# Attention in a new order: the products of x and of the output in one bank, queries ahead of the shifts, inputs transposed ahead of the probabilities

## The reference

```python
x = x + tanh(g_xattn) * xattn(layernorm(x), ctx)     # 16 heads of 8; rope on k and v; softmax; Wp, bp
x = x + tanh(g_ffn) * moe(layernorm(x))              # 8 experts, top 2 of a gate, hidden 256
# xattn: q = x Wq', k = rope(c Wk'), v = rope(c Wv'); softmax(q k' / sqrt(8)) v, then Wp' and + bp
# moe:   top 2 of x @ gate; softmax of the two; sum of weight * (silu(x w0) * (x w1)) @ wo
```

## Time and profile before

| | us |
|---|---|
| median of 3 executions | 569.37 (568.95 to 570.17) |
| profiled execution | 569.16 |
| its span | 567.4 |

### The profile page before, as it was taken

The page is one execution under the profiler, slowest core; times in us unless marked ns, Lnnn a source line. Parts: engine busy times, 40 slices in busy tenths (PEclk is TensorE's granted clock), DMA queues, the critical chain, the costliest instruction groups (busy, mean ns, idle before and its releaser), DMA issues.

```text
span 567.4 us, 20235 instructions
## 1 busy us (share of the span) xinstructions
PE 538.1 (95%) x5964; PEld 457.0 (81%) x5965; DVE 401.5 (71%) x1356; ACT 411.9 (73%) x1083; POOL 378.5 (67%) x520
## 2 busy tenths in 40 slices
PE   8999999999999999999999998799999999999960
PEld 6888887788887887887887878699999999999950
DVE  5888988898998899899899865433333333335763
ACT  4788888888888888889998885356666666666630
POOL 3236777767767677776776767777766666666770
PEclk9999999999999999999999999899999999999995
DMA  3832121121212212122221124333333333337997
GB/s 88 239 121 75 55 81 58 56 74 61 79 56 71 68 51 79 56 61 72 68 76 56 52 69 143 104 100 109 98 93 93 93 93 94 94 90 208 314 317 222
DMA packets 70246, 57.96 MB, mean 102 GB/s; under 512 B 8966, under 2 KB 66062, under 8 KB 70192
## 3 DMA queue, kind: packets, MB, share of 16 engines
q1 hardware_dynamic: 52672, 35.98, 22.3%
q0 software_dynamic: 8640, 16.93, 9.0%
q10 hardware_dynamic: 8880, 4.39, 2.6%
HBM read 29.84 MB, written 24.15 MB: 95 GB/s over the span
## 4 chain that ended last, share of the span: by engine, by line
PE 86%; issue 4%; POOL 3%; DMA 2%; DVE 2%; ACT 1%; POOLq 0%; SPq 0%; ACTq 0%; DVEq 0%
PE psH L548 18%; PE psO L520 12%; PE psH L460 11%; PE psH L446 7%; PE psH L452 7%; PE psK L498 5%; PE psO L562 5%; PE psG L562 4%; PE psO L478 3%; PE psX L465 3%; PE psO L492 3%; POOL results L1134 2%; PE psX L502 1%; PE psK L473 1%; PE psX L503 1%
## 5 line engine op out<-in xcount | busy, mean ns | idle before, releaser
L1134 POOL DMA_INDIRECT results<-ys,zin x142 | 141.9, 999 | 55.1 <-issue 51.0
L1085 POOL DMA_INDIRECT lists<-zp,dest x128 | 128.5, 1004 | 62.5 <-DVE dest L889 32.6
L548 PE MATMUL psH<-zT,wcur 128*128 128x256 f32 x568 | 136.0, 383 | 0.0
L548 PEld LDWEIGHTS psH<-zT,wcur 128*128 128x128 f32 x568 | 103.3, 192 | 11.4
L994 DVE TENSOR_TENSOR hm<-psH,hs 128x512 f32<-128x512 f32 x71 | 49.1, 692 | 85.9 <-PE psH L548 51.4
L627 ACT ACTIVATE ex<-psH,rs 128x512 f32<-128x512 f32 x128 | 81.2, 684 | 39.0 <-PE psH L452 39.0
L874 DVE TENSOR_REDUCE mx<-psH 128x8 fp32r<-128x512 f32 x128 | 82.4, 686 | 4.5 <-PE psH L446 0.3
L520 PEld LDWEIGHTS psO<-v,pT 128*64 128x64 f32 x2048 | 64.9, 138 | 25.1 <-issue 23.1
L460 PE MATMUL psH<-ident,ex 128*128 128x128 f32 x512 | 76.5, 282 | 0.1
L520 PE MATMUL psO<-v,pT 128*64 128x64 f32 x2048 | 73.7, 225 | 0.6 <-ACT pT L631 0.6
L1116 POOL TENSOR_TENSOR kvr<-ropA,ropB 128x256 f32<-128x256 f32 x64 | 46.5, 726 | 40.3 <-DVE ropB L951 24.0
(11 more groups left out here) (157 smaller groups left out, 991.6 us busy)
## 6 DMA issues: line engine op xcount, KB each, us to landing
zin<-lists SPq DMA_DIRECT2D x71, 130.0 KB, 2.1
yy<-results SPq DMA_DIRECT2D x16, 512.0 KB, 5.5
xres<-x1r SPq DMA_DIRECT2D x32, 128.0 KB, 2.2
out_dram<-xres ACTq DMA_DIRECT2D x16, 256.0 KB, 3.6
xring<-in_x_dram SPq DMA_DIRECT2D x31, 128.0 KB, 2.2
cring<-in_ctx_dram SPq DMA_DIRECT2D x31, 128.0 KB, 2.4
results<-ys,zin POOLq DMA_INDIRECT x142, 2.3
lists<-pad SPq DMA_DIRECT2D x16, 130.0 KB, 2.5
```

The costliest lines, as they stand in the source:

```text
L548: last = pe.matmul(bank[t.buf(2)][:, k * ET:(k + 1) * ET], wcur[:, t.buf(2), a, k * P:(k + 1) * P], zT[:, t.buf(2), :], start=True, stop=True)
L1085: nc.gpsimd.indirect_dma_start(lists, bass.IndirectOffsetOnAxis(ap=dest[:, t.buf(4), j:j + 1], axis=0), zp[:, t.buf(4), j, :], None).then_ ...
L1134: nc.gpsimd.indirect_dma_start(results, bass.IndirectOffsetOnAxis(ap=zin[:, t.buf(8), h, D:D + 1].bitcast(U32), axis=0), ys[:, t.buf(8), h ...
```

## The change

Nothing that is computed changes. Moved, on TensorE: the shift of half 1 goes from the end of a step to the next step, between the query product and the shift of half 0, so the query product now comes ahead of both shifts; the transposes of the inputs go from behind k and v to ahead of the probabilities' transposes; x·idg goes behind them; the output product goes behind k and v; the counting matmuls go ahead of P·V. Exchanged banks: x·idg and the output product write psG instead of psO; the transpose of `on` and the counting matmuls write psO instead of psG, beside P·V. So x·idg waits for x1_done of the tile before and no more for `on`, and P·V waits for the copy oT of the tile before in place of x1_done. On ACT the copy qT goes ahead of the exponentials, xcT from the end of the step to between oT and pT. On DVE the sum x1r goes from ahead of the rope products to between the reciprocal and `on`; each fourth step `place` stands there and the sum behind `on`. In the experts psY is exchanged so that the first tile uses psG.

```diff
-        psZ, psY = [psX, psK], [psO, psG]
+        psZ, psY = [psX, psK], [psG, psO]
@@ TensorE
-                    pe.matmul(psG[:, 384:384 + 4 * E], lower[:, :], chosen[:, :, :], start=True, stop=False)
-                    pe.matmul(psG[:, 384:384 + 4 * E], allone[:, :], before[:, :, :], start=False, stop=True).then_inc(place_ps, 4)
+                    pe.matmul(psO[:, 384:384 + 4 * E], lower[:, :], chosen[:, :, :], start=True, stop=False)
+                    pe.matmul(psO[:, 384:384 + 4 * E], allone[:, :], before[:, :, :], start=False, stop=True).then_inc(place_ps, 4)
...
+                    if t := ATT_PE.at(s, 2):
+                        if static(s, -2):
+                            busy(6)
+                        wait_for(pe, mx_done[1], t)
+                        shift(1)
                     if t := ATT_PE.at(s, 2):
                         wait_for(pe, mx_done[0], t)
                         shift(0)
...
                     if t := ATT_PE.at(s, 1):
                         wait_for(pe, on_done, t)
-                        if static(s, -1):
-                            pe.wait_ge(logit_ready, 4)
-                        pe.matmul(psO[:, 368:368 + XW], xcT[:, t.buf(8), 0:P], idg[:, :], start=True, stop=False, skip_group_check=True)
...
-                        pe.transpose(psG[:, 0:P], on[:, t.buf(2), :], ident[:, :]).then_inc(oT_ps, 1)
+                        pe.transpose(psO[:, 256:384], on[:, t.buf(2), :], ident[:, :]).then_inc(oT_ps, 1)
+                    if t := ATT_PE.at(s, 5):
+                        rows_in(pe, t)
+                        wait_for(pe, q_sb, t, back=1)
+                        pe.transpose(psX[:, 0:P], xring[:, t.buf(4), :], ident[:, :])
+                        pe.transpose(psX[:, P:2 * P], cring[:, t.buf(4), :], ident[:, :]).then_inc(xc_ps, 1)
+                    if t := ATT_PE.at(s, 1):
+                        if static(s, -1):
+                            pe.wait_ge(logit_ready, 4)
+                        wait_for(pe, x1_done, t, back=1)
+                        pe.matmul(psG[:, P:P + XW], xcT[:, t.buf(8), 0:P], idg[:, :], start=True, stop=False, skip_group_check=True)
                     if t := ATT_PE.at(s, 2):
                         wait_for(pe, exp_done[1], t)
                         turn(t, 1)
                     if t := ATT_PE.at(s, 2):
                         wait_for(pe, exp_done[0], t)
                         turn(t, 0)
-                    if t := ATT_PE.at(s, 1):
-                        wait_for(pe, oT_sb, t)
-                        pe.matmul(psO[:, 368:368 + XW], oT[:, t.buf(2), :], wTg[:, :], start=False, stop=True, skip_group_check=True).then_inc(attn_ps, 1)
                     if t := ATT_PE.at(s, 4):
...
                         pe.matmul(psK[:, 0:2 * D], xcT[:, t.buf(8), P:2 * P], wT[:, 1:3, :], start=True, stop=True).then_inc(kv_ps, 1)
-                    if t := ATT_PE.at(s, 5):
-                        rows_in(pe, t)
-                        wait_for(pe, q_sb, t, back=1)
-                        pe.transpose(psX[:, 0:P], xring[:, t.buf(4), :], ident[:, :])
-                        pe.transpose(psX[:, P:2 * P], cring[:, t.buf(4), :], ident[:, :]).then_inc(xc_ps, 1)
+                    if t := ATT_PE.at(s, 1):
+                        wait_for(pe, oT_sb, t)
+                        pe.matmul(psG[:, P:P + XW], oT[:, t.buf(2), :], wTg[:, :], start=False, stop=True, skip_group_check=True).then_inc(attn_ps, 1)
...
                         scores(t, 0)
+                    if (t := ATT_PE.at(s, 0)) and t.buf(4) == 3 and not static(s, NT - 1):
+                        places(t)
...
                     if t := ATT_PE.at(s, 2):
                         wait_for(pe, v9_done, t)
-                        wait_for(pe, x1_done, t, back=1)
+                        wait_for(pe, oT_sb, t, back=1)
...
                         last.then_inc(pv_ps, 1)
-                    if (t := ATT_PE.at(s, 0)) and t.buf(4) == 3 and not static(s, NT - 1):
-                        places(t)
...
-                    if t := ATT_PE.at(s, 3):
-                        if static(s, -3):
-                            busy(6)
-                        wait_for(pe, mx_done[1], t)
-                        shift(1)
@@ ScalarE
+                    if t := ATT_ACT.at(s, 0):
+                        wait_for(act, q_ps, t)
+                        wait_for(act, s_ps[0], t, back=2)
+                        nc.scalar.copy(qT[:, t.buf(2), :], psX[:, 2 * P:3 * P]).then_inc(q_sb, 1)
                     if t := ATT_ACT.at(s, -2):
                         wait_for(act, shift_ps[1], t)
...
-                    if t := ATT_ACT.at(s, 0):
-                        wait_for(act, q_ps, t)
-                        wait_for(act, s_ps[0], t, back=2)
-                        nc.scalar.copy(qT[:, t.buf(2), :], psX[:, 2 * P:3 * P]).then_inc(q_sb, 1)
                     if t := ATT_ACT.at(s, -3):
                         wait_for(act, oT_ps, t)
                         wait_for(act, attn_ps, t, back=2)
-                        nc.scalar.copy(oT[:, t.buf(2), :], psG[:, 0:P]).then_inc(oT_sb, 1)
+                        nc.scalar.copy(oT[:, t.buf(2), :], psO[:, 256:384]).then_inc(oT_sb, 1)
+                    if t := ATT_ACT.at(s, 1):
+                        wait_for(act, xc_ps, t)
+                        wait_for(act, attn_ps, t, back=8)
+                        nc.scalar.copy(xcT[:, t.buf(8), :], psX[:, 0:2 * P]).then_inc(xc_sb, 1)
                     if t := ATT_ACT.at(s, -2):
                         wait_for(act, p_ps[1], t)
...
-                    if t := ATT_ACT.at(s, 1):
-                        wait_for(act, xc_ps, t)
-                        wait_for(act, attn_ps, t, back=8)
-                        nc.scalar.copy(xcT[:, t.buf(8), :], psX[:, 0:2 * P]).then_inc(xc_sb, 1)
@@ VectorE
+                def first_sum(t):
+                    wait_for(dve, attn_ps, t)
+                    wait_for(dve, zn_done, t, back=4)
+                    wait_slot(dve, [x1_out[i // 2] for i in range(4)], t, 16, back=4)
+                    nc.vector.tensor_tensor(x1r[:, t.buf(4), :], psG[:, P:P + XW], bpg[:, :], ALU.add).then_inc(x1_done, 1)
...
                         nc.vector.reciprocal(rden[:, :], o[:, :, DH]).then_inc(rden_done, 1)
+                    r = (r if (r := ATT_DVE.at(s, -1)) and r.buf(4) == 3 else None)
+                    if r:
+                        rows(r)
+                    elif t := ATT_DVE.at(s, 0):
+                        first_sum(t)
+                    if t := ATT_DVE.at(s, 1):
+                        o = psO[:, 0:PAIRS * VW].rearrange("p (h w) -> p h w", w=DH + 1)
                         wait_for(dve, rden_done, t)
...
+                    if r and (t := ATT_DVE.at(s, 0)):
+                        first_sum(t)
```

More of the change, by code:

```diff
@@ L429, in places @@
                     wait_for(pe, place_done, t, back=4)
-                    pe.matmul(psG[:, 384:384 + 4 * E], lower[:, :], chosen[:, :, :], start=True, stop=False)
-                    pe.matmul(psG[:, 384:384 + 4 * E], allone[:, :], before[:, :, :], start=False, stop=True).then_inc(place_ps, 4)
+                    pe.matmul(psO[:, 384:384 + 4 * E], lower[:, :], chosen[:, :, :], start=True, stop=False)
+                    pe.matmul(psO[:, 384:384 + 4 * E], allone[:, :], before[:, :, :], start=False, stop=True).then_inc(place_ps, 4)
                 def count():
-                    pe.matmul(psG[:, 0:E], allone[:, :], before[:, 0, :], start=True, stop=True).then_inc(count_ps, 1)
+                    pe.matmul(psO[:, 416:416 + E], allone[:, :], before[:, 0, :], start=True, stop=True).then_inc(count_ps, 1)
                 def busy(n):
@@ L795, in first_table @@
                         dve.wait_ge(count_ps, 1)
-                        nc.vector.tensor_scalar(early[:, 0, :], psG[:, 0:E], 0.0, None, ALU.add).then_inc(early_table, 1)
+                        nc.vector.tensor_scalar(early[:, 0, :], psO[:, 416:416 + E], 0.0, None, ALU.add).then_inc(early_table, 1)
                         dve.wait_ge(early_table, 1)
@@ L824, in second_table @@
                         dve.wait_ge(count_ps, 2)
-                        nc.vector.tensor_copy(cnt[:, :], psG[:, 0:E]).then_inc(late_table, 1)
+                        nc.vector.tensor_copy(cnt[:, :], psO[:, 416:416 + E]).then_inc(late_table, 1)
                         dve.wait_ge(late_table, 1)
@@ L937, in attention_step @@
                         nc.vector.tensor_tensor(chosen[:, :, :], oh[:, :, 0, :], oh[:, :, 1, :], ALU.add).then_inc(chosen_done, 4)
-                    if t := ATT_DVE.at(s, 0):
-                        wait_for(dve, attn_ps, t)
-                        wait_for(dve, zn_done, t, back=4)
-                        wait_slot(dve, [x1_out[i // 2] for i in range(4)], t, 16, back=4)
-                        nc.vector.tensor_tensor(x1r[:, t.buf(4), :], psO[:, 368:368 + XW], bpg[:, :], ALU.add).then_inc(x1_done, 1)
                     if t := ATT_DVE.at(s, 3):
```

16 lines of the change are left out of this document (8 added, 8 removed).

## The result

| us | before | after |
|---|---|---|
| median | 569.47 (568.95 to 570.17, 4 executions) | 589.16 (588.97 to 590.97, 4 executions) |
| ratio | 1 | 1.0352, interval 1.0329 to 1.0375 |
| span of the profiled execution | 567.4 | 587.4 |

The change costs 19.7 us. Forecast were 11.6 us, 580.8, with a range up to 589.0. So the direction came as forecast, and the size did not: the time lies just beyond the upper end. Three later sets of runs took about 93 us longer (663 us) with every kernel, the one before too, so their numbers stand apart, under 8 of the experiments.

A forecast was written before the change was run, and what follows sets the result against it. The prediction took ACT's exponentials, then TensorE's own queue, to bound the attention step. It summed 569.2 + 3.6 (ordinary steps) + 8.0 (counting matmuls) = 580.8 us, range 571 to 589.

The forecast's parts named there:

- The bound: Attention step of 5.01 us: ACT's exponentials set it up to the second transposes, TensorE's queue behind; their 0.16 stall stays.
- Queries ahead of the shifts: TensorE, attention: the query product now delays the shift of half 1, +0.22 us a step.
- Inputs ahead of the probabilities: TensorE, attention: 0.22 leaves the paid stretch, only 0.16 got back; period 5.07, +0.06 a step, +3.6 to 3.8 us.
- xcT ahead of pT: ACT, attention: the second copy pT starts 0.00 to 0.03 us later; upper end 0.25 a step without overlap.
- Counts ahead of P·V: TensorE, every fourth step: counting matmuls wait for GpSimd's `before`, 0.61 or 0.45 us a group, 8.0 in all.
- my split into eight and seven: Counting groups in attention: eight cost 0.61 us each and seven 0.45, from earlier slack of 0.51 or 0.67.
- The start: No term of its own; remaining terms of either sign, under 1.5 us, were set to zero.
- Banks, `on`: TensorE, attention: x·idg stops waiting for `on`, whose transpose waits about 0.1 us instead, under the exponentials; gain nothing.
- The sum x1r: DVE, attention: moved behind the reciprocal, it makes `on` up to 0.04 us later, under the exponentials; costed at nothing.
- Experts: Experts' phase: order kept, psO and psG exchanged, cost 0.
- rival 3: ACT, attention: no overlap, pT 0.25 us later each step; 592 us, half of it 586; larger loss, chance 0.13.
- the count's own upper end: Counting groups in attention: GpSimd's chain not earlier, 0.23 us more each, 11.5 in all instead of 8.0.

The follow-up runs named there:

- 8 of the experiments: Eight timings of kernels with parts of the change or related edits, beside a kernel before of 662 to 663 us; all slower than it by 1 to 4%.
- experiment 1: The kernel after, with the counting matmuls back behind P·V and writing psK: 577.82 us, ratio 1.0152.
- experiment 2: The kernel after, with ACT's copy xcT back behind the two copies pT: 587.05 us, ratio 1.0313.
- experiment 3: The kernel after, with both the counting matmuls back behind P·V (into psK) and xcT behind pT: 575.14 us, ratio 1.0118.
- experiment 4: The kernel before, with only the query product ahead of both shifts and its copy qT ahead of the exponentials: 585.22 us, ratio 1.0282.
- experiment 5: The kernel before, with only the exchanged banks, x·idg behind the transpose of `on` and the moved sum x1r; counts behind P·V in psK: 571.8 us, ratio 1.0039.
- experiment 6: The kernel before, with only the counting matmuls moved ahead of P·V: 582.77 us, ratio 1.025.

## Why the prediction was right or wrong

- *The bound.* Right. The stall of 0.16 ahead of the second transposes is there in the ordinary steps of the kernel after as in those of the one before, and in experiments 1 to 6.
- *Queries ahead of the shifts, +0.22.* Right: 0.23 alone (experiment 4).
- *Inputs ahead of the probabilities, 0.16 of 0.22 got back, period 5.07.* Right: 5.07 stands in experiments 2 and 3, where xcT is out of the way.
- *xcT ahead of pT, 0.00 to 0.03, taken at nothing in the sum.* Mis-sized: this is the first step that failed. It costs 0.07 in each ordinary step (5.14 with it, 5.07 without, experiment 2). pT starts at +2.09 (reckoned +2.07); the second copy starts 0.04 later than before, near what I reckoned, but also takes 0.63 instead of 0.59, and ends at +3.19 to +3.20 instead of +3.13. Behind the exponential of half 0 ACT had no slack, and TensorE waits for ACT's last copy in each ordinary step, so every hundredth there is paid; the steps with a count are as long without it (experiment 2). Over the 44 steps: 5.61 measured, 2.6 forecast (44 × 0.06), 3.0 too little. Experiment 2 gives 2.25 of the 3.0 back; most of the rest lies in the steps behind a count, as in experiment 3.
- *Counts ahead of P·V, 0.61 and 0.45 a group.* The mechanism is right, place and releaser too; the sizes are short, and this is the second step that failed. Against the kernel before I forecast 0.67 and 0.51 more per counting step and measured 0.80 in both kinds, up to 1.1 in the last groups (6.54 instead of 5.40). Of what is missing (0.13 and 0.29), 0.09 to 0.12 are that P·V comes 0.21 to 0.24 behind the count, not 0.15, and q 0.03 later. In five of the 15 groups the count's load comes 0.23 behind the end of `before` and not 0.07, 0.16 more (in one other, 0.12). The timelines call that "issue"; the records of TensorE's own queue (line 104, `wait_for`), which they leave out, show why the two kinds differ. In the five groups a register operation (ALU_OP, at 194.40 in one) stands between the end of the wait for `before` (194.34) and the load (194.49); in the others none does, and the load follows the end of the wait by 0.025. The cheaper kind of my split into eight and seven has only these five groups. Sum: 12.40 measured, 8.9 forecast (15 × 0.59), 3.5 too little.
- *The start.* Not forecast: a term that I put at nothing. At the fifth tile the kernel after is 2.05 late, of which four steps of the forecast 0.06 explain 0.24. 0.93 lie in these four steps, most of it in the first, 5.54 instead of 4.87; experiment 4 has 5.52 there, so that goes with the queries ahead of the shifts. The other 1.12 lie before the first shift, and can be chance: kernels that start like the one before have it anywhere from 12.34 to 13.90, and one and the same kernel (the counts alone) at 12.34, 13.09 and 13.68.
- *Banks, `on`, 0.* Right: the ordinary step is 5.01 in experiment 5. *The sum x1r, 0.* Wrong in part: moved ahead of `kmask`, it costs 2.0 us alone and about 0.7 in experiment 3, in the steps behind a count. In the change the wait for pT hides most of it.
- *Experts, 0.* Right: the last shift is 20.07 later, the span 20.0.

The forecast by parts was 2.6 + 8.9 + 0.24 = 11.7. Measured were 5.6 + 12.4 + 2.05 = 20.1. The three misses (3.0, 3.5, 1.8) all have the same sign, which my range hadn't allowed for: its upper end came from rival 3 at half its price, and from the count's own upper end. Rival 3 (pT 0.25 later) holds in kind and falls in size: 0.07 to 0.10.

The Trainium skill, TensorEngine Tiling (Array Packing), Key Properties, has TensorE drain when the tiling mode changes. No run here can show a price for that. The load of the other shape comes 0.21 to 0.24 behind the count and the load of the same shape 0.04, but between the count and P·V the queue also passes two waits of P·V's own, which elsewhere pass while the scores run, and in every group P·V loads 0.025 behind the end of the second. So what I had too small there may well be the queue's time for two waits, and that the rows agree with the rule, as the prediction says, isn't shown.

## What to carry to other kernels

Ask of each move not only what it costs, but in which stretch of the step the instruction stands: the same 0.22 of TensorE is free under the exponentials, as long as there is slack, and paid in full behind them. A small instruction that waits for a slow engine belongs behind everything that others wait for; two counting matmuls ahead of P·V cost 11 to 13 us of 569. And where a copy on the path has no slack, give its neighbours their full price: errors of some hundredths in a loop of 60 add up, and here they all lay on one side.

## What the runs showed of the hardware that I had not expected

- Two semaphore waits that stand between two matmuls in TensorE's queue go with a gap even when little or nothing has to be waited for: P·V's load came mostly 0.21 to 0.24 us behind the count's, in experiment 6 and in the kernel after alike, and in every group 0.025 behind the end of the second wait. In the last group of the kernel after the waits ended later, and so came the load, 0.31 behind. Whether the changed shape of the array has a part in it can't be told apart here; I had reckoned 0.15 from rows of the inputs' transposes.
- A load that was held by a semaphore came 0.07 us behind the releasing instruction where the wait was the last thing in the queue ahead of it, and 0.23 where a register operation for the next wait stood between, in both kernels with the counts ahead.
- A copy of the same size took 0.63 us instead of 0.59 in the changed order on ACT (the second copy pT, in the loop's steps of the kernel after and of experiment 1), and again 0.59 once xcT stood behind it. Why wasn't looked into.
